# Longer runs of filler products on TensorE in the routing stage of a one-core kernel

## What is computed

```python
y = irfft(rfft(u_m, n=2*L) * rfft(kernel, n=2*L), n=2*L)[..., :L]
y = (y + u_m * D[:, None]) * mask[:, None, :]
probs = softmax(y.reshape(-1, H) @ gate_w.T)
vals, idx = top_k(probs, 2)                      # w: the two weights of a token, normalised
h = silu(y @ g.T) * (y @ u.T)                    # 16 experts of 112 hidden units each
out = x + einsum('bei,hei,be->bh', h, d_r, w)
```

## Time and profile before

| | us |
|---|---|
| median of three runs | 499.8 (499.45 to 500.56) |
| the profiled execution, its own time | 496.27 |
| span of the profiled execution, first to last instruction | 494.2 |

### The profile page before, as it was taken

How to read it: one execution, slowest core, us unless ns; L and a number is a source line. 1 busy time by engine, 2 the same in 40 slices (tenths; PEclk the granted TensorE clock), 3 DMA queues, 4 the chain that set the end, 5 groups by cost and what they waited for, 6 DMA issues and landing times.

```text
span 494.2 us, 9023 instructions
## 1 busy us (share of the span) xinstructions
PE 435.8 (88%) x2834; PEld 381.2 (77%) x2834; DVE 195.8 (40%) x512; ACT 100.9 (20%) x229; POOL 177.6 (36%) x217
## 2 busy tenths in 40 slices
PE   0359999989999998895969999999999999999991
PEld 0359998879899898884958887888887788888770
DVE  6924344333444432639613333333333333333330
ACT  3870000000001000011012222222222232222220
POOL 4542332222222200005685334446344354552322
PEclk9989999999999999997899999999999999999997
DMA  8966898989889998899584897997997796775541
GB/s 282 341 204 191 283 265 269 287 261 276 279 284 304 306 295 261 284 387 350 151 299 86 261 285 169 277 273 205 285 250 209 213 278 154 152 159 97 86 71 20
DMA packets 46490, 115.98 MB, mean 235 GB/s; under 512 B 10098, under 2 KB 25714, under 8 KB 46322
## 3 DMA queue, kind: packets, MB, share of 16 engines
q1 hardware_dynamic: 25138, 73.49, 45.5%
q0 software_dynamic: 12096, 33.58, 29.8%
q10 hardware_dynamic: 9216, 8.39, 5.5%
HBM read 93.63 MB, written 40.66 MB: 272 GB/s over the span
## 4 chain that ended last, share of the span: by engine, by line
PE 58%; DMA 23%; SPq 6%; DVE 6%; issue 2%; POOL 2%; ACT 0%; another core or an unknown queue 0%; ACTq 0%; POOLq 0%; DVEq 0%
PE conv_ps L1052 25%; DMA k_rows<-k_sb 17%; PE conv_ps L1071 14%; PE conv_ps L939 9%; PE turn_ps L1061 7%; DMA arena<-k_rows 4%; SPq L312 4%; SPq L311 3%; PE conv_ps L1033 2%; DVE tmp L622 1%; DMA ys<-y_rows,from_row 1%; PE conv_ps L1078 1%; POOL arena L429 1%; PE turn_ps L950 1%; DMA out<-arena,from_row 1%
## 5 line engine op out<-in xcount | busy, mean ns | idle before, releaser
L939 PE MATMUL conv_ps<-arena 128*128 128x256 f32 (+7 forms) x1024 | 157.1, 310 | 12.7 <-DMA arena<-k_rows 12.3
L939 PEld LDWEIGHTS conv_ps<-arena 128*128 128x128 f32 x1024 | 148.8, 192 | 20.6 <-issue 8.5
L1052 PE MATMUL conv_ps<-arena,ys_t 128*128 x640 | 127.8, 353 | 3.8 <-DVE ys_t L886 3.8
L1052 PEld LDWEIGHTS conv_ps<-arena,ys_t 128*128 128x128 f32 x640 | 118.1, 190 | 15.5 <-issue 15.5
L456 POOL DMA_INDIRECT out<-arena,from_row x40 | 62.9, 1572 | 119.9 <-DMA out<-arena,from_row 82.3
L1071 PE MATMUL conv_ps<-arena,hid_t 112*128 x160 | 75.7, 595 | 1.0 <-DVE hid_t L901 1.0
L727 DVE TENSOR_TENSOR arena<-conv_ps,mask_t 128x256 f32<-128x256 f32 x64 | 27.0, 424 | 98.6 <-PE conv_ps L939 97.7
L894 DVE TENSOR_TENSOR hid<-silu,conv_ps 128x112 f32<-128x112 f32 x40 | 10.9, 272 | 102.1 <-ACT silu L576 98.4
L906 DVE TENSOR_SCALAR arena<-conv_ps,slot_weight 128x512 f32<-128x512 f32 x40 | 30.0, 751 | 42.7 <-PE conv_ps L1071 41.7
L385 POOL TENSOR_TENSOR am<-wave,cs_re 128x128 f32<-128x128 f32 x16 | 6.5, 406 | 108.8 <-ACT wave L518 105.4
L1071 PEld LDWEIGHTS conv_ps<-arena,hid_t 112*128 112x128 f32 x160 | 27.2, 190 | 21.0 <-issue 20.8
(11 more groups left out here) (149 smaller groups left out, 369.6 us busy)
## 6 DMA issues: line engine op xcount, KB each, us to landing
arena<-k_rows SPq DMA_DIRECT2D x64, 512.0 KB, 6.6
arena<-gu_t SPq DMA_DIRECT2D x16, 896.0 KB
y_rows<-y_blk ACTq DMA_DIRECT2D x64, 128.0 KB, 3.1
arena<-x_time SPq DMA_DIRECT2D x56, 128.0 KB, 5.3
arena<-d_t SPq DMA_DIRECT2D x16, 448.0 KB
arena<-x_time SPq DMA_DIRECT2D x2, 512.0 KB, 6.0
out<-arena,from_row POOLq DMA_INDIRECT x44
out<-ys SPq DMA_DIRECT2D x1, 512.0 KB, 7.4
```

The lines of the kernel that those rows point to most:

```text
L939: last = nc.tensor.matmul(conv_ps[:, h, d * B:C * B], toep[:, p, h, d * P:(d + 1) * P], u_t[:, p, h, 0:(C - d) * B], start=(d == 0), stop= ...
L1052: last = nc.tensor.matmul(gu_ps, ys_t[:, t % 2, c, :], flat[:, bass.ds(bufs[t] * WE + c * GU, GU)], start=(c == 0), stop=(c == C - 1))
```

## The change

It touches TensorE's program alone, in four places. The 30 fillers before the first piece become 46. Two fillers are issued ahead of the products of each of the last three pieces, behind that piece's waits. Behind the table the 20 fillers stay; after them come a wait for `sources_made` and 20 further fillers, and only then turn(0).

```diff
-            stay_awake(30, k_bank[:, :, :])
+            stay_awake(46, k_bank[:, :, :])
 
             for q, (lo, hi) in enumerate(PIECES):
                 pe.wait_ge(hot_row_made, q + 1)
                 pe.wait_ge(hot_weight_made, q + 1)
                 pe.wait_ge(hot_token_made, q + 1)
+                if q in (2, 3, 4):
+                    stay_awake(2, k_bank[:, :, :])
                 for j in range(lo, hi):
                     last = nc.tensor.matmul(table_ps, slot_row[:, j, :], slot_tile[:, j, :],
                                             start=(j == 0), stop=(j == K * G - 1))
             last.then_inc(table_made, 1)
 
             stay_awake(20, k_bank[:, :, :])
+            pe.wait_ge(sources_made, 1)
+            stay_awake(20, k_bank[:, :, :])
```

## The result

The changed kernel takes 506.5 us (median of four runs, 503.6 to 508.7) against 499.6 for the kernel before: a ratio of 1.014, 95% interval 1.008 to 1.020. It is slower by 6.9 us, not by 2.7. The profiled execution took 506.47 us with a span of 504.4.

What follows compares the result with a forecast made beforehand. TensorE's expert stage was taken as the bound, so turn(0)'s 2.74 us delay, with the table 0.27 us later and 80 filler records taking 8.95 us, reaches the end: 499.8 + 2.7 = 502.5 us, range 499.9 to 504.2.

Steps and rivals of the forecast that it cites:

- What bounds the kernel: Expert stage: TensorE is always busy from 264 to 478 us, so a later start moves the end equally.
- Part 1: Before the first piece: 16 more fillers, 3.6 us, hidden in 5.05 us idle; clock stays at 1.00.
- that rival: Table pieces: clock falls between them, pieces end 1.1 us later, 3.8 us in all, 503.6 to 505.6; chance 0.08.
- Part 2: Table pieces: fillers hidden in pieces 2 and 3, 0.45 us on the path in the last; table 0.27 us later.
- Part 3: Behind the table: the wait costs nothing, the added 20 fillers delay turn(0), from 248.21 to 250.95, by 2.74 us.
- Both runs follow each other without a gap: 80 records x 0.112: Between table and turn(0): 40 fillers take 8.95 us from 242.0, so turn(0) starts at 250.95.
- absorbed by the stall in tile 1: Turn(1): a 2.0 us stall tied to a time hides most of the delay, 0.7 us left, 500.5; chance 0.16.
- 0.2% for what a measurement can tell: Whole kernel: a measurement tells about 0.2%, 1.0 us, from no change.
- The "faster" rival: First gather lands 2.7 us later in timed runs, fillers save 3 us of half clock: 496.8; chance 0.12.
- modelled tails of 0.275 us: Filler runs before the first piece: 0.275 us taken off the 6.86 us to get 0.112 us per record.

Runs made afterwards that it cites:

- parts 1 and 2 together: Kernel before with 46 fillers before the first piece and two ahead of pieces 2, 3 and 4, the 20 behind the table unchanged: ratio 1.0005.
- part 3 without them: Kernel before with only the wait for sources_made and 20 further fillers added behind the table's 20 fillers: ratio 1.014.
- the paced pair: Gathers paced: two, empty scatters, two, then two for each of four tiles; kernel before 495.1 us (0.9915), changed kernel 497.6 us (0.997).
- second profile of the kernel before: The kernel before, run again unchanged for a second profile: ratio 0.995, profiled execution 498.52 us.
- the run with four gathers: Changed kernel with four gathers before the four empty scatters in place of eight, and four tiles ahead from there: ratio 1.047.
- the last probe ahead of turn(0): Changed kernel plus four products with own semaphores between last filler and turn(0); the fourth, a transpose of gathered rows, signalled at 15.19 us; no ratio given.

## Why the prediction was wrong

**What bounds the kernel** held: a later start of the expert stage arrives at the end. **Part 1** held as to the cost of its fillers. The clock didn't stay at 1.00 between the pieces: it fell at 230.79 for 6.83 us, and piece 2 took 3.26 us. I had given that rival 0.08 and 1.1 us in front of the gather, 3.8 in all. It came in eleven of the twelve profiles with parts 1 and 2, and the gather stands 1.2 us further behind GpSimd's last copy than in the first profile (5.07 for 3.89), close to its price; so its chance was set far too low. It doesn't carry the loss: parts 1 and 2 together measured 1.0005, part 3 without them 1.014, and two profiles of the unchanged kernel are as late at this point (5.0 and 5.3). **Part 2** measured as summed where the clock held, 0.3 us. In its sum the 2.9 us between two pieces are 2.55 for the last, which changes nothing, as 2.25 still fit in.

**Part 3** had the right sign and one right term: turn(0) is recorded 2.5 us later than without it (7.11 for 4.62 in the kernel with parts 1 and 2 alone; 2.74 forecast, of which 0.27 stood in front of the gather), and the paced pair measures a loss of this size by itself. **The step that failed** is "Both runs follow each other without a gap: 80 records x 0.112". In the records the sentence came true, 80 without a gap; in the work it didn't. I took the end of the last record for the end of the work and put the time from there to the semaphore at nothing, in a stretch in which eight gathers land. The missing term is 6.4 us from the record of turn(0) to its signal. The pace had been read from a stretch without gathers, though not without transfers (the 60 fillers of the earlier trace rows; no semaphore tells whether they kept pace):

```profile
217.89:224.75 6.86, 6.86 (x61) 1.00 1.17 436
```

Against the second profile of the kernel before, gate_up(1) starts 7.8 us later (23.2 for 15.4): 2.7 for turn(0)'s record, 6.3 more for its signal, 0.9 for the rest of the half clock in gate_up(0), less 2.15 for the stall of turn(1) that is now spared. By gate_up(2) 6.1 are left, since gate_up(1) was at half clock there; the medians say 6.9.

**The rival "absorbed by the stall in tile 1"** (0.16) had the evidence in hand and read it backwards. I had seen transposes that are signalled 2.0 us behind their records, and took them for an event tied to a time which a later turn would miss. It is work of TensorE that lags while eight gathers land, and a change that moves more dense work into that stretch makes it longer. The forecast also took 0.2% for what a measurement can tell; the interval of the result is 0.6% to either side, and the unchanged kernel came out 0.5% from itself. The "faster" rival, with the gather landing later, didn't come: the first gather lands 4.4 to 4.7 us behind its issue in every profile in which turn(0) waits for it.

The Trainium skill (Perfetto Trace Analysis, Tensor Engine Instruction (MATMUL, LD_WEIGHTS)) says that the profiler's start of a product is the start of its operand prefetch, that its end is computed and not observed, and that the semaphore moves only when the writes to PSUM are acknowledged. The trace agrees, 8.15 for the computed end against 14.57 for the signal. I had written of modelled tails of 0.275 us and not asked how far off a modelled end can be.

**What stays open.** Why dense weight loads and products fall behind while the gathers' rows are written is not shown; gate_up(0) of the kernel before, at 0.20 us per record, ran in the same traffic and was signalled on time (10.04), so it is no plain limit on records per microsecond. Nor is it the amount of rows written, as the run with four gathers shows. Every execution timed here was recorded by the profiler, and the recording loses entries in this very stretch: of the 16 steps that a gather's semaphore makes, the list has 2 to 9 for each of the fourth to the eighth gather of the burst, and 14 to 16 in the kernels that start with two or four. Whether the recording takes part in the lag can't be told from these runs. The Trainium skill (DMA: Bandwidth & Descriptors, Back-pressure in remote DMA) says that a saturated port of SBUF clogs the path back to the DMA engines; it speaks of DMA between cores, and no run here tests it for TensorE.

## What to carry to other kernels

A filler is free only if it ends before the wait it covers, and "ends" means its semaphore, not its record: put a semaphore on the last one, or look at when the consumer of the next product starts. While a burst of DMA lands, keep short products away, use few long ones (512 columns) or none, and issue the first gathers of a stage at the pace at which they are needed. Here the paced gathers gave 0.6 to 0.9%, where all care for the clock in the gap gave nothing that could be measured. Long fillers took away most of the lag's price, not that of the fillers themselves (1.005).

## What the runs showed of the hardware that I had not expected

- TensorE's completions lag its records by up to 7.3 us (7.94 and 15.19, the last probe ahead of turn(0)) while eight gathers of 512 KB land, with 128-column products at 0.112 us per record; with 512-column products in their place it is 0.01 to 0.02 us.
- The lag ends about when the burst does: the last row in the traces is written at 14.4 to 16.4 us behind the issue of the first gather, and the last held product is signalled at 12.9 in one profile and at 14.4 to 16.1 in all others, with no filler in front, with 20 or with 40.
- With two gathers in flight turn(0) lags by 0.01 us, with four by 0.75, with eight by 6.4, behind the same 40 fillers.
- Without a filler behind the table the clock fell and tile 0 ran at half speed, and the time was not higher for it (ratio 0.997, 0.994 to 1.000).
- Ten executions of the unchanged kernel in one run lay between 494.2 and 502.3 us; its medians of 10 and 12 runs came out at 0.995 and 1.003 of the kernel before.
